# Third attention: one query product for two batches, in three buffers, placed among the key and value products

## The reference, cut to what matters

```
x = x + _L2_xattn_ref(_layernorm(x), ctx_1024, Wq, Wk, Wv, Wo, bo)
def _L2_xattn_ref(x, context, Wq, Wk, Wv, Wo, bo):     # H, DH = 16, 64
    q = (x @ Wq.T).reshape(b, nq, H, DH)               # Wq: 1024 x 256
    k = (context @ Wk.T).reshape(b, nk, H, DH)
    v = (context @ Wv.T).reshape(b, nk, H, DH)
    sim = jnp.einsum('bihd,bjhd->bhij', q, k) * DH ** -0.5
    attn = jax.nn.softmax(sim, axis=-1)
    out = jnp.einsum('bhij,bjhd->bihd', attn, v).reshape(b, nq, H * DH)
    return out @ Wo.T + bo
```

## Time and profile before

| | us |
|---|---|
| median of 3 runs (2300.58 to 2303.03) | 2302.82 |
| the profiled execution: its time | 2305.7 |
| its span in the trace | 2303.8 |
| TensorE busy | 2166.2 (94%) |
| VectorE busy | 1284.7 (56%) |
| ScalarE busy | 1074.2 (47%) |

### The profile page before, as it was taken

How to read it: one execution, slowest core, us unless ns; L and a number is a source line. 1 busy time by engine, 2 the same in 40 slices (tenths; PEclk the granted TensorE clock), 3 DMA queues, 4 the chain that set the end, 5 groups by cost and what they waited for, 6 DMA issues and landing times.

```text
span 2303.8 us, 46633 instructions
## 1 busy us (share of the span) xinstructions
PE 2166.2 (94%) x16038; PEld 1756.0 (76%) x16038; DVE 1284.7 (56%) x3563; ACT 1074.2 (47%) x2929; POOL 447.7 (19%) x478
## 2 busy tenths in 40 slices
PE   8999989999988899999999999999959979999998
PEld 6888877777756667678788888888746758888888
DVE  6888863222244522556556556555542238888766
ACT  5888871222123132244444444444402228888863
POOL 3122101111153344100000000000014432121160
PEclk9999999999999799999999999999969989999999
DMA  8777746222264322110000000001221247787601
GB/s 213 196 198 197 182 107 263 92 92 76 68 196 151 130 68 67 42 46 8 20 27 16 12 8 19 12 8 49 96 108 62 65 127 177 203 194 191 172 19 33
DMA packets 154868, 230.65 MB, mean 100 GB/s; under 512 B 66609, under 2 KB 127489, under 8 KB 152337
## 3 DMA queue, kind: packets, MB, share of 16 engines
q1 hardware_dynamic: 142160, 196.07, 30.2%
q0 software_dynamic: 10656, 29.37, 4.1%
q10 hardware_dynamic: 1824, 2.23, 0.3%
HBM read 176.36 MB, written 51.25 MB: 99 GB/s over the span
## 4 chain that ended last, share of the span: by engine, by line
PE 83%; DVE 7%; issue 4%; ACT 2%; DMA 2%; POOL 1%; SPq 1%; ACTq 0%; DVEq 0%; POOLq 0%
PE bank L1157 10%; PE bank L2020 9%; PE bank L1188 7%; PE bank L2053 6%; PE bank L1043 6%; PE bank L1039 6%; PE bank L2085 6%; PE bank L1083 4%; PE bank L1142 4%; PE bank L1135 4%; PE bank L1028 4%; PE bank L2070 3%; PE bank L1056 2%; PE bank L2406 2%; PE bank L2420 2%
## 5 line engine op out<-in xcount | busy, mean ns | idle before, releaser
L1157 PE MATMUL bank<-ident,arena 112*125 112x112 f32 x2352 | 375.0, 277 | 2.3 <-DVE arena L1395 0.3
L1157 PEld LDWEIGHTS bank<-ident,arena 112*125 112x125 f32 x2352 | 341.6, 190 | 32.3 <-ACT arena L1428 5.9
L1428 ACT ACTIVATE arena<-arena,mx 112x375 f32<-112x375 f32 x512 | 309.3, 605 | 104.0 <-DVE mx L1374 101.3
L1374 DVE CUSTOM_DVE_ANT_0 arena<-bank,maskf 112x375 f32<-112x375 f32 x512 | 273.4, 543 | 83.4 <-PE bank L1135 78.5
L1428 ACT ACTIVATE arena<-bank,mx 112x375 f32<-112x375 f32 x272 | 155.1, 574 | 182.4 <-DVE mx L1386 155.4
L2020 PE MATMUL bank<-arena 128*128 x532 | 229.8, 555 | 2.2 <-ACT arena L2146 2.1
L1395 DVE COPY arena<-bank 125x336 f32<-125x336 f32 x448 | 214.5, 503 | 17.2 <-PE bank L1157 17.2
L1135 PE MATMUL bank<-kS,qS 128*112 128x376 f32 x512 | 203.8, 399 | 16.1 <-DMA qS<-query_halves 13.1
L1188 PE MATMUL bank<-arena 125*32 125x112 f32 (+1 forms) x4608 | 202.8, 265 | 3.1 <-DVE arena L1395 2.9
L1188 PEld LDWEIGHTS bank<-arena 125*32 125x32 f32 (+1 forms) x4608 | 144.5, 118 | 49.9 <-issue 32.5
L2053 PE MATMUL bank<-arena 128*128 (+1 forms) x672 | 167.1, 380 | 0.0
(11 more groups left out here) (266 smaller groups left out, 3679.2 us busy)
## 6 DMA issues: line engine op xcount, KB each, us to landing
kS<-key_halves SPq DMA_DIRECT2D x256, 188.0 KB, 3.9
key_halves<-arena SPq DMA_DIRECT2D x64, 376.0 KB, 4.2
arena<-in_ctxT SPq DMA_DIRECT2D x62, 376.0 KB, 3.8
arena<-in_f_out SPq DMA_DIRECT2D x21, 768.0 KB, 4.4
qS<-query_halves SPq DMA_DIRECT2D x252, 56.0 KB, 3.1
arena<-in_f_up SPq DMA_DIRECT2D x4, 2816.0 KB, 19.9
arena<-results SPq DMA_DIRECT2D x38, 224.0 KB, 4.6
query_halves<-arena SPq DMA_DIRECT2D x32, 224.0 KB, 3.6
```

Of the source, the lines that this page charges most:

```text
L1157: m = pe.transpose(bank[2 + g % 2][0:KT, k * S:(k + 1) * S], pr[:, g % t.NR, k * KT:(k + 1) * KT], ident[0:S, 0:S])
L1374: dve.tensor_tensor_reduce(sm[:, g % 2, :], bank[g % 2][0:S, 0:SK], maskf[:, :], -t.a["scale"], 3e38, ALU.add, ALU.min, mx[:, g % t.NR:g % ...
L1428: act.activation(pr[:, g % t.NR, :], src, ACT.Exp, bias=mx[:, g % t.NR:g % t.NR + 1], scale=-1.0, accum_out=row_sum(t, b)[:, h:h + 1]).the ...
```

## The change

Queries are made for two batches at once (`QB = 2`): a query product now takes two of the eight blocks of output columns (`QG = 2`) and moves 224 columns, the 112 of batch b and the 112 of batch b + 1. Four such products, q0 to q3, make the queries of an even batch and the odd one behind it. They stand in the odd windows only, and ahead of the first window for batches 0 and 1. The other attentions have two blocks, so `QG` was 2 there already.

In every window of the third attention the extras now begin with k0 and v0. In odd windows q0 follows, then k1, v1, q1, k2, v2, q2, k3, o, k4, v3, q3 and the rest. The planned cost of one query product is 0.45 x 2.

Each query product is copied out by two instructions (one for each batch) on ScalarE and two on VectorE, of 128 x 224 each, where it was one of 128 x 448. The query halves have three buffers, taken by `b % 3`. Room for them comes from `mid`, now a part of the arena, from 448 columns behind the context halves, and from `sm`, which this attention does not use.

```diff
-        self.QG = min(4, self.NO)
+        self.QG = 2
+        self.QB = 2 if self.halves else 1
...
-        q = [(gen("q", o), 0.45 * self.QG, 0) for o in range(0, self.NO, self.QG)]
+        q = [(gen("q", o), 0.45 * self.QG, 0) for o in range(0, self.NO, self.QG) if b % self.QB == 0]
...
-            return (q + k[0:1] + v[0:1] + k[1:2] + v[1:2] + k[2:3] + v[2:3] + k[3:4] + out + k[4:5] + v[3:4] + k[5:6]
-                    + v[4:5] + k[6:7] + v[5:6] + k[7:8])
+            return (k[0:1] + v[0:1] + q[0:1] + k[1:2] + v[1:2] + q[1:2] + k[2:3] + v[2:3] + q[2:3] + k[3:4] + out
+                    + k[4:5] + v[3:4] + q[3:4] + k[5:6] + v[4:5] + k[6:7] + v[5:6] + k[7:8])
...
+        queries_2 = lambda b, half, o, n: qH[b % 3 * 2 + half][o // 4][:, o % 4:o % 4 + n, :]
...
+                    N = t.QB * S
                     for j in range(t.QG):
                         for c in range(ND):
-                            m = pe.matmul(dst[:, j * S:(j + 1) * S], w[0][:, c, (o + j) * P:(o + j + 1) * P],
-                                          xnT[:, c, b * S:(b + 1) * S], start=(c == 0), stop=(c == ND - 1))
+                            m = pe.matmul(dst[:, j * N:(j + 1) * N], w[0][:, c, (o + j) * P:(o + j + 1) * P],
+                                          xnT[:, c, b * S:b * S + N], start=(c == 0), stop=(c == ND - 1))
...
                         if h == 0:
-                            freed_all(pe, t, "q", b)
+                            freed_all(pe, t, "q", b - b % t.QB)
...
-                        ins = dve.scalar_tensor_tensor(out=qH[:, b % 2, 1, o:o + t.QG, :],
-                                                       in0=src[:, 0:t.QG * S].rearrange("p (o t) -> p o t", t=S),
-                                                       scalar=qscale, in1=qH[:, b % 2, 0, o:o + t.QG, :].bitcast(F32),
-                                                       op0=ALU.mult, op1=ALU.subtract)
+                        both = src[:, 0:t.QG * 2 * S].rearrange("p (o e t) -> p o e t", e=2, t=S)
+                        for e in range(2):
+                            ins = dve.scalar_tensor_tensor(out=queries_2(b + e, 1, o, t.QG), in0=both[:, :, e, :],
+                                                           scalar=qscale,
+                                                           in1=queries_2(b + e, 0, o, t.QG).bitcast(F32),
+                                                           op0=ALU.mult, op1=ALU.subtract)
...
-                        ins = act.activation(qH[:, b % 2, 0, o:o + t.QG, :],
-                                             src[:, 0:t.QG * S].rearrange("p (o t) -> p o t", t=S), ACT.Copy,
-                                             scale=-t.a["scale"])
+                        both = src[:, 0:t.QG * 2 * S].rearrange("p (o e t) -> p o e t", e=2, t=S)
+                        for e in range(2):
+                            ins = act.activation(queries_2(b + e, 0, o, t.QG), both[:, :, e, :], ACT.Copy,
+                                                 scale=-t.a["scale"])
```

More of the change, by code:

```diff
@@ L88 @@
 SLOT1 = 4488
-ARENA = WF_AT + 2 * SLOT1
+MID_AT = WF_AT + 2 * SLOT1
+ARENA = MID_AT + 8 * S
 VPAD = NKT * 16 * 32
@@ L563, in build @@
         kH = within(KT_AT, "key_halves_2", [P, 2, 8, SKE], F32R)
-        qH = within(QM_AT, "query_halves_2", [P, 2, 2, 8, S], F32R)
+        QH_AT = [[QM_AT + (2 * n + half) * 8 * S + part_ * 4 * S for part_ in range(2)]
+                 for n in range(2) for half in range(2)] + [[MID_AT, MID_AT + 4 * S], [2 * ND * SKE, SM_AT]]
+        qH = [[within(at, f"query_halves_2_{n}{part_}", [P, 4, S], F32R) for part_, at in enumerate(both)]
+              for n, both in enumerate(QH_AT)]
+        queries_2 = lambda b, half, o, n: qH[b % 3 * 2 + half][o // 4][:, o % 4:o % 4 + n, :]
         slotR = [within(TAB_AT + 17 * 128, f"slot_ids{L}", [P, 2 * B * EVEN], F32R) for L in (1, 2)]
@@ L620, in build @@
         hg = oT[:, 0:2 * 512].rearrange("p (b n) -> p b n", b=2)
-        mid = sb("mid", [P, 2, TOK])
+        mid = part(MID_AT, 2 * TOK).rearrange("p (b n) -> p b n", b=2)
         wR = sb("wR", [P, ND, E])
@@ L1141, in att_tensor @@
                                 rows = slice(j * dh, (j + 1) * dh)
-                                m = pe.matmul(bank[j][0:S, 0:SKE], qH[rows, b % 2, qh, h // 2, :], kH[rows, kh, h // 2, :],
+                                m = pe.matmul(bank[j][0:S, 0:SKE], qH[b % 3 * 2 + qh][h // 8][rows, h // 2 % 4, :], kH[rows, kh, h // 2, :],
                                               start=(n == 0), stop=(n == 2))
```

## The result

The changed kernel took 2356.84 us (median of 4 runs, 2356.01 to 2357.72) against 2302.93 (4 runs, 2300.58 to 2303.21): ratio 1.0240, 95% interval 1.0228 to 1.0252, slower by 53.9 us. The forecast was 2351, slower by 48.6, with 2329 to 2372 as its range for 8 in 10. The profiled execution took 2356.0 us, with a span of 2354.2.

A forecast was written before the change was run, and what follows sets the result against it. TensorE's work laid end to end was taken as the third attention's bound. Profiled 2305.7 us, plus 30.6 (stalls and copies less width and old holes), plus 18 for the clock, less 2.9 to the median: 2351 us, range 2329 to 2372.

The forecast's parts named there:

- Waits for the context halves: Window starts: TensorE's k0 waits for VectorE to finish the context halves, fifteen stalls of 2.4 to 3.5 us, +45.1 us.
- The step that decides: With query products gone from the window's head, k0 comes first and TensorE stands still until the halves end: 45.1 us.
- Width: Query products on TensorE: 32 of 224 columns at 1.61 us replace work of 58.7 us, saving 7.2 us.
- Old holes: Six TensorE waits before query products for a bank-freeing copy vanish, -8.3 us; two clock falls with them, -3.0.
- Copies of half size: Query copies in two halves free banks later: v4 waits 0.5 us in seven odd windows, 3.5; start 0.5.
- The clock: TensorE's clock falls behind twelve of the fifteen stalls, 1.5 us each: +18 us, bounds 0 and 51.
- the two idle times over 3 us: TensorE idle times of 3.60 and 3.17 us in the profile before, both followed by granted clock 0.50.
- Rival A: The clock holds: all stalls at k0 but no clock falls, +30.6, 2333 us; chance 0.18.
- Rival B: Every stall brings the clock down for long, fifteen falls of 2.9 us in the mean: +74, 2377 us; chance 0.12.
- Rival C: Faster: VectorE has the context halves ready when k0's turn comes, -14.5, 2288 us; chance 0.05.
- Rival D: ScalarE or VectorE becomes the bound of odd windows; would add to the forecast; no chance of its own.
- the estimated 107 ns a record: Query products: 128 weight columns at 1.2 GHz by the skill's weight-load rule, said to save 6 us, not 7.2.

The follow-up runs named there:

- experiment 1: Kernel before with only the extras reordered, k0, v0, q0 first in every window, old query products kept: 2368.51 us, ratio 1.0291 to the kernel before.
- experiment 5: experiment 1's kernel with a second buffer of context halves, made eight slots earlier: 2293.62 us, ratio 0.9965 to the kernel before.
- experiment 6: Kernel before with only the router product two slots later, no longer between a window's two query products: 2289.70 us, ratio 0.9953 to the kernel before.
- experiment 3: Changed kernel with six useless TensorE products ahead of each k0's wait, overwritten by k0: 2332.32 us, ratio 1.0133 to the kernel before.
- experiment 2: Changed kernel with q0 and q1 ahead of k0 in odd windows, even windows still beginning with k0: 2329.53 us, ratio 1.0122 to the kernel before.

## Why the prediction was right, and where it was off

- *Waits for the context halves*: worked out as 45.1 us in fifteen, measured 45.1 in fifteen, 2.5 to 3.5 each. The step that decides is right in its mechanism and its size: the product at the head hid VectorE's chain. Experiments 1 and 5 show that the cause is the halves' readiness and nothing else in the order: with the wait 67 us are lost, without it 7 are won.
- *Width*: forecast -7.2. Taken from one start to the next, waits left out, the 32 old products' 512 records cost 61.8 us, of which 2.3 are the low clock in windows 3 and 7; experiment 6, without these, has 58.9. The 256 new records take 51.0. So the term is about -8. It was a little undersized, since some of the wide products run into the next group at 1.37 us.
- *Old holes*: -8.3 and both falls gone, as forecast.
- *Copies of half size*: v4 waits seven times, 2.8 us in all (forecast 3.5); the start costs 0.1 and not 0.5.
- *The clock*: this is the term that was mis-sized. Twelve falls at 1.5 were forecast, +18; there were fifteen in fifteen, and experiment 3 puts them at 23.1 to 24.5, about 1.6 each. No row gave the number twelve: it was picked between none and fifteen, and that it came out near is in part luck. The six holes of up to 1.45 us, of which two brought it down, were no measure for waits of 2.4 to 3.5; the two idle times over 3 us were the better one. The sum with the measured terms is 45.1 + 2.8 + 0.1 - 8 - 8.3 - 3.0 + 24.5 = +53, against 53.9 between the medians and 53.3 inside the stage; with 23.6 for the clock it is +52. Experiment 6, which takes away the old holes and their two falls alone, bears out -8.3 and -3.0: it gains 11.25. The two profiled executions differ by less, 50.3 us: behind the last window, outside this sum, the output product ran for 6.50 us in that of the kernel before, for 5.26 in the changed one's and for 3.68 in experiment 6's, by how long the clock was low there.
- *Rival A*, the clock holds, is refuted, and with it the Trainium skill's bound as a guard for this kernel. By its page "TensorE: Matmul & The Clock Gate", section "HAM oscillation — how this bites in real kernels", which warns of idle times beyond a bound, the fourteen waits of 2.5 to 3.1 us would be harmless. Each of them brought the clock down, and the measurement decides. The prediction says that the bound lies above all the stalls it forecasts; the 3.5 us of window 1 do not lie below it. *Rival B* was half right in kind: the low stretches were short here but for window 1, and longer in six of eight in experiment 2. *Rival C* would have needed halves that are ready when k0's turn comes; experiment 5 made them so, and with that order only then it is faster. *Rival D*: VectorE and ScalarE have less to do per unit of time than before (VectorE 342.96 us of the 614, where it had 361.59).
- *Sums of the prediction that do not come out*, none of which the forecast hangs on: with the estimated 107 ns a record the saving would be 512 x 0.107 - 51.5, about 3 us, and not 6. The own range of the forecast, by the falls and the 4 us that it names, is 2340 to 2360 and not 2341 to 2364; the result lies in both. TensorE's busy share was forecast at about 92% and is 93.3% (572.57 of 614).

## What to carry to other kernels

Ask of work that is to be moved what it hides where it stands. An instruction list that shows no wait at an edge may owe that to the very products in front of it: follow the other engine's chain from the last common point to the edge, and what is left when the cover is taken away is the price, here right in the sum to a tenth of a microsecond. Then add the clock. In these runs TensorE stood still for the context halves 39 times for 2.5 to 3.5 us (15, 15, 8 and 1 times in the changed kernel and experiments 1, 2 and 5), and 39 times the clock fell: in a stage that TensorE fills count a fall each time.

## What the runs showed of the hardware

Six useless matrix products ahead of each wait made the whole kernel 23 to 24.5 us (1%) faster, because TensorE's granted clock stayed at 1.00 through fifteen waits behind which it otherwise stood at 0.50.

How long the clock stays low after such a wait is not fixed: with waits of the same 3.1 us it was mostly the short stretch in the changed kernel and mostly one twice as long in experiment 2. The traces show what goes with it, the moment of the fall. In window 2 of the changed kernel the clock was still at 1.00 while TensorE stood idle, and fell 0.9 us after k0 had begun. In window 4 of experiment 2 it was at 0.50 while TensorE still stood idle, 1.6 us before k0 began at 1174.60, and stayed there through the work behind:

```profile
1173.50:1174.00 0.50, 0.00 (x0) 0.00 (x0) 0.49 (x1) 0.00 (x0) 0.00 (x0) 0.50 0.05 16
...
1175.00:1179.00 4.00, 4.00 (x12) 3.25 (x11) 0.55 (x1) 0.48 (x1) 0.00 (x0) 0.50 0.00 0
```

All 39 waits sort this way: the eleven falls that came 0.7 us or more before k0 (once in the changed kernel, four times in experiment 1, six in experiment 2) have the long low stretch, the 28 that came later the short one. What sets the moment of the fall wasn't tried. Nor does the spread of the runs show it: experiment 2's lie within 9.6 us, but those of the kernel before beside it lie within 11.5.
